# Preln linear-attention layer plus tensor-train FFN on 8 cores: stores on arrival, a shared unfold, and GpSimd's order within a slot

## The chip, the cores and the metric

The kernel runs on the 8 NeuronCores of one Trainium2 chip (trn2) as one launch. No core writes what another reads. The metric is device microseconds of the slowest core; less is better. One execution of the kernel before was profiled on all cores, and three more were timed.

## The reference, cut to what matters

Input `x` is (4, 4096, 1024) in float32. Layer norm, then an attention block with a recurrent state, a residual add, layer norm, a complex linear map whose weights come from a tensor-train product, and a second residual add:

```python
mixed = einsum('btd,cd->btc', ln(x), W_qkv)          # 3072 channels
mixed = silu(causal_conv4(mixed))                    # 4 taps per channel
q, k, v = split(mixed); q = l2norm(q) * HD**-0.5; k = l2norm(k)
z = ln(x) @ W_z.T
beta = sigmoid(ln(x) @ W_b.T)
g = -exp(A_log) * softplus(ln(x) @ W_a.T + dt_bias)
# per head and token: S = S*exp(g) + k (v*beta)^T ;  o = q S
out = rmsnorm(o) * silu(z)
x = x + out @ W_out.T
W_real = reshape(einsum('abcd,cefg->abefdg', G1_R, G2_R))   # 512 x 512, "unfold"
W_imag = reshape(einsum('abcd,cefg->abefdg', G1_I, G2_I))
x = x + [xr@W_real.T - xi@W_imag.T + br,  xr@W_imag.T + xi@W_real.T + bi]   # of ln(x)
```

## The kernel before, in words

**Who does what.** A core pair shares one of the four sequences of 4096 tokens. The even core (0, 2, 4, 6) owns the first five tiles of 512 tokens (NPRE=0, NOWN=5). The odd core first runs over the same five tiles for keys, values and state only (NPRE=5) and then owns the last three (NOWN=3). `emit(NPRE, NOWN)` builds both programs. I speak of even and odd cores.

**Slots.** The main loop runs over tiles `t` from -1 and four slots `s` in each. In a slot the core streams tile `u = t+1` (projection of a chunk of channels, the 4-tap convolution as four matmuls with diagonal blocks, SiLU), and works on chunk `n` (128 tokens) of tile `t`: decay matrix (`decay`), scores (`qk`), output (`oT`), state update (`state`). One slot later (`n1`) come `gate_out` and `outproj`, two slots later (`n2`) `ln2_norm`, `add_bias`, `ffn` and `y_store`. A slot of an even core has 7 projections and 7 convolutions (slots 0 to 2 of a tile), or 3 of both and 8 z projections (slot 3). A slot of an odd core before its own tiles has 4 and 4. The last four slots of tile `NT-1` and two more stream nothing: I call them the tail.

**Order.** Every engine takes its instructions in program order; waits are written out by hand as tokens (`need`). So the order of the calls in the slot body is the order on VectorE (`V`), GpSimd (`G`), ScalarE (`S`), TensorE (`P`) and on SyncE's DMA queue (`Y`). A `Y.need` or `G.need` holds everything that is behind it in that queue.

**Weights.** `w_uses` lists the uses of the 32 weight blocks (128x1024) in order. Five buffers `s_w` (NW=5) rotate. `w_issue(i)` loads use `i`. At the first use of a block it is a GpSimd DMA from the float32 `wcat`, which converts to bf16; it waits for the projection that last used the buffer and for the buffer's store (`q_ws`). After its first use the block lives in the bf16 scratch `wscr`, and SyncE loads it from there. `w_keep(i)` (L389) makes the store into `wscr`. In `proj(u, cc, j)` and `zproj` the order is: projection `i`, `w_keep(i)`, `w_issue(i + NW)`, then the copy of PSUM to `s_pre` (ScalarE for odd `j`, L527; VectorE for even `j`, L530). With five buffers, the load for the 7th projection of a slot is issued behind the 2nd.

**Diagonal blocks.** The same scheme with six buffers `s_d` (ND=6): at first use VectorE builds the block (L386) once the convolution that last used the buffer and the buffer's store are done. `d_keep(i)`, called behind convolution `i` (L553), stores it to `dscr`; later uses load it from there. Both stores are on SyncE's queue.

**Norms.** `ln1_norm(m)` makes the normalised rows of the tile two ahead (L431, VectorE, float32 to bf16), lets SyncE transpose them by DMA into `s_lnxT` (L140) and loads the next rows (`x_load`, 512 KB). In the slot it comes behind the fourth projection.

**Unfold.** `unfold()` builds the FFN weights `s_wbig` on VectorE: 2 parts (real, imaginary) of 4 row chunks, each 4 products (L977), 3 sums (L985) and 2 copies (L990 to L996), 72 instructions of 128x512. They are float32 but for the copies. `uf(RATE)` puts RATE of them behind each projection from slot 1 of the first tile on; RATE is 3 on even, 1 on odd cores. `xr_load` and `ffn` wait for the last one.

**GpSimd in a slot**, in order: the stores of `r_act` (row scales to `rscr`), the causal mask of the first half (`affine_select`, L756, in `decay(n,0)`), the squares of q (`s_qsq`, L791, inside `qtil`), `r_load` (two DMAs that broadcast `rscr` into `s_rb`, behind a wait for the stores), the mask of the second half, `add_bias` (L945), the state's decay (L839), small DMAs, and late in the slot the copy of the state (L875). VectorE's `gate_out` (L897) waits for `s_rb`; `outproj` waits for `gate_out` and for `s_og` (L826).

Of the kernel before, what the change touches and what calls it, by code (L numbers as in the profile page):

```python
# [8 lines left out]
ALU = mybir.AluOpType  # L9
# [139 lines left out]
def build_program():  # L149
# [93 lines left out]
    facc = x2[1][:, 512:1024]  # L243
    ftmp = x2[2][:, 0:512]
# [36 lines left out]
    def emit(NPRE, NOWN):  # L281
# [87 lines left out]
        def w_keep(i):  # L369
            u, cc = w_uses[i]  # L370
            if wscr_tok.get(cc) is None:
                Y.need(w_tok[i])
                wscr_tok[cc] = q_ws[i % NW].go(Y, wscr[cc], wr[i % NW])

        def d_issue(i):
# [8 lines left out]
            else:  # L384
# [5 lines left out]
                dscr_tok[cc] = None  # L390

        def d_keep(i):
            u, cc = d_uses[i]
            if dscr_tok.get(cc) is None:
# [113 lines left out]
        def proj(u, cc, j):  # L508
# [12 lines left out]
            w_keep(i)  # L521
# [23 lines left out]
        def conv(u, cc, j):  # L545
# [7 lines left out]
            d_keep(i)  # L553
# [13 lines left out]
        def zproj(u, cc):  # L567
            i, k, ps, t = proj_mm(u, cc)
            proj_tok[(u, cc)] = t
            w_keep(i)  # L570
# [212 lines left out]
        def qtil(n):  # L783
# [5 lines left out]
                                                 in1=eb[:, :, sl], op=ALU.mult))  # L789
            G.need(silu_tok[(t, 7)], ss_tok.get(n - 1))  # L790
# [98 lines left out]
        def r_load(n):  # L889
            G.need(q_r[0].tok, q_r[1].tok, gat_tok.get(n - 1))  # L890
# [10 lines left out]
        def xr_load(n):  # L901
            if n >= 4 * NOWN:
                return
            Y.need(yst_tok.get(n - 3), ffnw[0])
# [43 lines left out]
        def ffn(n):  # L948
            P.need(*psA_free[0])
            P.need(l2_tok[n], ffnw[0])  # L950
# [16 lines left out]
        def unfold():  # L967
            toks = [cload(Y, ft1[0], d_t1[0]), cload(Y, ft1[1], d_t1[1]),
                    cload(Y, ft2[0], d_t2[0]), cload(Y, ft2[1], d_t2[1])]
            V.need(*toks)  # L970
            t = None
            for k in range(2):
                for rc in range(4):
                    a = ft1[k][:, rc * 128:(rc + 1) * 128]
                    for c in range(4):
                        V.need(t)
                        t = V.mark(V.e.tensor_tensor(  # L977
                            out=(facc if c == 0 else ftmp).rearrange("p (b e) -> p b e", b=32),
                            in0=a[:, c * 32:(c + 1) * 32, None].broadcast_to([128, 32, 16]),
                            in1=ft2[k][:, None, c * 16:(c + 1) * 16].broadcast_to([128, 32, 16]),  # L980
                            op=ALU.mult))
                        yield
                        if c > 0:
                            V.need(t)
                            t = V.mark(V.e.tensor_tensor(out=facc, in0=facc, in1=ftmp,  # L985
# [31 lines left out]
        ffnw = [None]  # L1017
# [32 lines left out]
        for t in range(-1, NT + 1):  # L1050
            for s in range(NCH):
# [58 lines left out]
                if on2:  # L1110
                    ln2_norm(n2)
# [106 lines left out]
```

How the kernel before makes its waits and increments, by code:

```python
    def mark(self, ins):  # L110
        ins.then_inc(self.h, 1)
        self.v += 1
        return (self, self.v)
# [1 line left out]
    def need(self, *toks):  # L115
        for tok in toks:
            if tok is None:
                continue
            src, val = tok
            if val <= 0 or self.seen.get(src.name, 0) >= val:
                continue
            self.e.wait_ge(src.h, val)
            self.seen[src.name] = val
# [10 lines left out]
    def go(self, lane, out, in_):  # L134
        lane.e.dma_start(out=out, in_=in_).then_inc(self.h, 16)
        self.v += 16
        return (self, self.v)
# [1 line left out]
    def gotr(self, lane, out, in_):  # L139
        lane.e.dma_start_transpose(out=out, in_=in_).then_inc(self.h, 16)
        self.v += 16
        return (self, self.v)
# [122 lines left out]
    def begin(eng, name, out, in_):  # L265
        eng.dma_start(out=out, in_=in_).then_inc(sem(name), 16)
        begun.add(name)
```

## Time and profile before

| what | value |
|---|---|
| runs of the kernel before | 893.12, 892.51, 887.84 us; median 892.51 |
| the profiled execution's own time | 892.11 us |
| its span, slowest core (core 2, even) | 890.2 us |
| spans, even cores 0, 2, 4, 6 | 888.1, 890.2, 886.6, 879.7 us |
| spans, odd cores 1, 3, 5, 7 | 882.8, 886.2, 887.3, 881.4 us |
| core 2, busy | PE 77%, VectorE 55%, ScalarE 33%, GpSimd 30% |
| core 2, DMA | 129 MB, mean 145 GB/s |

The span runs from a core's first to its last instruction; the execution's own time is 1.9 us above the span of the slowest core. Times in the rows are microseconds from the start of the core's span. PE is TensorE, DVE VectorE, ACT ScalarE, POOL GpSimd, SPq SyncE's DMA queue. "PEclk" is TensorE's granted clock as a share of full speed, "DMA share" the mean busy share of 16 DMA engines. In a row of the timeline the bracket holds the idle time of the engine before the instruction and what ended it. DMA-issuing rows show the issue, not the transfer.

### The profile page before, as it was taken

What the parts mean: (1) busy time and instruction counts of PE and PEld (TensorE: products, weight loads), DVE (VectorE), ACT (ScalarE), POOL (GpSimd) and SP (SyncE); (2) the same over time, 40 slices, a digit from 0 to 9 for tenths busy, and PEclk for the clock granted to TensorE, in tenths of its full rate; (3) what the DMA queues carried; (4) which work ended last, traced back from release to release, by engine and by line L of the source; (5) the groups of instructions that cost most, each with busy time, mean ns of one, the idle gap of its engine ahead of it and who ended that gap; (6) DMA issues with size and microseconds to landing.
All of it is one profiled execution on the core that took longest, in us unless ns stands there. A gap on an engine that the chain in (4) does not pass through costs nothing.

```text
span 890.2 us, 14242 instructions; the slowest of 8 cores (879.7 to 890.2 us)
## 1 busy us (share of the span) xinstructions
PE 686.3 (77%) x4687; PEld 316.4 (36%) x4767; DVE 487.2 (55%) x678; ACT 296.8 (33%) x522; POOL 266.9 (30%) x317
## 2 busy tenths in 40 slices
PE   0768674689887979979897997897999897665543
PEld 0323231234343424434343443443444443332211
DVE  4537784245656365666546657633465453656532
ACT  1143340246434325433434444413543343111100
POOL 2122111033324150450514315325044152334410
PEclk9998896799998989999899999989999999766668
DMA  9598986876366663744746456365374464122222
GB/s 195 118 238 168 182 198 184 200 205 188 78 181 171 156 175 100 203 129 152 193 132 193 122 176 168 105 169 136 116 190 105 106 163 109 41 77 67 84 59 63
DMA packets 102223, 129.00 MB, mean 145 GB/s; under 512 B 48382, under 2 KB 65284, under 8 KB 102016
## 3 DMA queue, kind: packets, MB, share of 16 engines
q1 hardware_dynamic: 88272, 99.38, 39.2%
q0 software_dynamic: 13872, 28.63, 16.7%
q8 instruction: 42, 0.69, 0.3%
q14 instruction: 37, 0.30, 0.1%
HBM read 107.40 MB, written 22.76 MB: 146 GB/s over the span
## 4 chain that ended last, share of the span: by engine, by line
PE 53%; DMA 20%; DVE 11%; issue 7%; ACT 4%; SPq 2%; POOL 2%; DVEq 0%; ACTq 0%; POOLq 0%
PE pR L503 20%; PE pR L550 9%; PE pB L912 9%; PE pA L953 7%; DMA dscr<-s_d 6%; DMA s_w<-wscr 5%; DMA wscr<-s_w 3%; DMA s_rb<-rscr 3%; DVE s_ln L935 2%; SPq L140 1%; DMA s_i128b<-i 1%; PE pB L807 1%; DMA rscr<-s_r 1%; PE pB L813 1%; DVE s_ktil L728 1%
## 5 line engine op out<-in xcount | busy, mean ns | idle before, releaser
L503 PE MATMUL pR<-s_lnxT,s_w 128*128 128x512 bf16 x1240 | 314.7, 405 | 73.2 <-DMA s_w<-wscr 27.3
L503 PEld LDWEIGHTS pR<-s_lnxT,s_w 128*128 128x128 bf16 x1280 | 126.9, 102 | 239.7 <-issue 115.7
L550 PE MATMUL pR<-s_pre,s_d 128*128 128x512 bf16 x460 | 117.1, 386 | 15.7 <-DVE s_pre L530 9.3
L135 POOL DMA_DIRECT2D rscr<-s_r x40 | 22.2, 558 | 267.4 <-ACT s_r L884 92.1
L912 PE MATMUL pB<-s_wout,s_gated 128*128 128x512 bf16 x308 | 80.7, 416 | 23.5 <-DVE s_og L826 11.6
L556 ACT ACTIVATE s_post<-pR 128x512 bf16<-128x512 f32 x120 | 68.9, 593 | 64.1 <-PE pR L550 63.6
L530 DVE CAST s_pre<-pR 128x512 bf16<-128x512 f32 x70 | 48.0, 688 | 70.1 <-PE pR L503 70.1
L918 DVE TENSOR_TENSOR s_x<-pB,s_x 128x1024 f32<-128x1024 f32 x20 | 24.5, 1225 | 101.2 <-PE pB L912 101.2
L953 PE MATMUL pA<-s_wbig,s_ln2T 128*128 128x512 bf16 x312 | 73.2, 384 | 6.6 <-DMA s_ln2T<-s_ln 6.1
L550 PEld LDWEIGHTS pR<-s_pre,s_d 128*128 128x128 bf16 x480 | 41.6, 98 | 64.5 <-issue 19.7
L527 ACT CAST s_pre<-pR 128x512 bf16<-128x512 f32 x50 | 29.3, 585 | 96.2 <-PE pR L503 96.1
L573 ACT ACTIVATE s_zT<-pR 128x512 bf16<-128x512 f32 x40 | 23.7, 597 | 110.2 <-PE pR L503 100.3
L912 PEld LDWEIGHTS pB<-s_wout,s_gated 128*128 128x128 bf16 x320 | 33.2, 106 | 66.9 <-issue 36.8
L875 POOL CAST s_Sb<-s_S 128x512 bf16<-128x512 f32 x20 | 12.2, 608 | 146.3 <-DVE s_ssb L870 146.3
L556 ACT ACT_TABLE_LOAD x20 | 25.7, 1283 | 77.6 <-PE pR L550 77.6
L756 POOL TENSOR_SCALAR_AFFINE_SELECT s_dsb<-s_dsb 128x1024 bf16<-128x1024 bf16 x40 | 44.4, 1110 | 23.6 <-ACT s_dsb L752 23.1
L414 ACT ACT_TABLE_LOAD x21 | 26.9, 1283 | 71.1 <-DVE s_pre L480 58.5
L135 POOL DMA_DIRECT2D s_w<-wcat x31 | 17.2, 557 | 101.0 <-DMA wscr<-s_w 38.8
L953 PEld LDWEIGHTS pA<-s_wbig,s_ln2T 128*128 128x128 bf16 x320 | 31.3, 99 | 44.6 <-issue 8.3
L958 DVE TENSOR_TENSOR s_x<-pA,s_x 128x1024 f32<-128x1024 f32 x20 | 24.5, 1225 | 41.1 <-PE pA L953 41.1
L945 POOL TENSOR_TENSOR s_x<-s_x,s_biasb 128x1024 f32<-128x1024 f32 x20 | 42.6, 2129 | 14.2 <-DVE s_ln L935 14.2
L897 DVE TENSOR_TENSOR s_gated<-s_og,s_rb 128x1024 bf16<-128x1024 bf16 x20 | 25.0, 1250 | 29.5 <-DMA s_rb<-rscr 29.5
(118 smaller groups left out, 891.7 us busy)
## 6 DMA issues: line engine op xcount, KB each, us to landing
s_w<-wscr SPq DMA_DIRECT2D x128, 256.0 KB, 4.6
s_d<-dscr SPq DMA_DIRECT2D x96, 128.0 KB, 3.4
s_x<-x SPq DMA_DIRECT2D x22, 512.0 KB, 5.7
s_rb<-rscr POOLq DMA_DIRECT2D x40, 256.0 KB, 4.7
y<-s_x SPq DMA_DIRECT2D x20, 512.0 KB, 2.9
s_xa<-x SPq DMA_DIRECT2D x18, 512.0 KB, 6.4
s_w<-wcat POOLq DMA_DIRECT2D x32, 256.0 KB, 6.2
wscr<-s_w SPq DMA_DIRECT2D x32, 256.0 KB, 5.6
```

The costliest lines, as they stand in the source:

```text
L135: lane.e.dma_start(out=out, in_=in_).then_inc(self.h, 16)
L414: t = S.mark(S.e.activation(out=bn[:, 14:15], in_=bn[:, 13:14], func=AF.Ln, bias=EPS5))
L503: ins = P.e.matmul(ps, w[:, dc * 128:(dc + 1) * 128], lnxT[u % 2][:, dc, :], start=(dc == 0), stop=(dc == 7))
L527: te = S.mark(S.e.copy(out=pre[:, j, 3:515], in_=ps))
L530: te = V.mark(V.e.tensor_copy(out=pre[:, j, 3:515], in_=ps))
L550: ins = P.e.matmul(ps, dr[i % ND][:, tap * 128:(tap + 1) * 128], pre[:, j, tap:tap + 512], start=(tap == 0), stop=(tap == 3))
L556: silu_tok[(u, cc)] = ring_free[k] = S.mark(S.e.activation(out=post[u % 2][:, cc, :], in_=ps, func=AF.Silu))
L756: exp_tok[(n, h2)] = G.mark(G.e.affine_select(out=d3, in_=d3, pattern=[[0, 8], [1, 128]], compare_op=ALU.is_ge, fill=zero_reg, base=0, cha ...
L897: gat_tok[n] = V.mark(V.e.tensor_tensor(out=gated.rearrange("p (a b) -> p a b", a=8), in0=og.rearrange("p (a b) -> p a b", a=8), in1=rb, o ...
L912: ins = P.e.matmul(pB[:, hf * 512:(hf + 1) * 512], gated[:, cc * 128:(cc + 1) * 128], wout[:, cc, hf * 512:(hf + 1) * 512], start=(cc == 0 ...
L945: xb_tok[n] = G.mark(G.e.tensor_tensor(out=x2[n % 3], in0=x2[n % 3], in1=biasb, op=ALU.add))
L953: ins = P.e.matmul(pA[:, hf * 512:(hf + 1) * 512], ln2T[n % 2][:, dg, :], wbig[:, dg, hf * 512:(hf + 1) * 512], start=(dg == 0), stop=(dg ...
```

## The change

Five edits.

1. `d_keep` is gone: the block is stored to `dscr` right behind its building, in `d_issue`.
2. `w_keep` is called two uses ahead (`i + 2`) in `proj` and `zproj`, and for uses 0 and 1 before the first norms.
3. `unfold(L, k)` is now one generator for each part: part 0 on VectorE, part 1 on GpSimd, with buffers of their own (part 1 borrows half of an `s_x2` buffer and half of `s_rb`). `uf` steps both. RATE for even cores is 2. The loads of its inputs are issued at the end of slot 0. `r_load`, `xr_load` and `ffn` wait for both parts.
4. `ln1_norm` moves from behind the fourth projection to directly behind `ln2_norm`, between the first and the second projection.
5. GpSimd's squares of q leave `qtil` and become `q_squares`, called behind `qk(n, 1)`; `add_bias` is moved there too, behind them.

```diff
-    facc = x2[1][:, 512:1024]
-    ftmp = x2[2][:, 0:512]
+    facc = [x2[1][:, 512:1024], x2[2][:, 512:1024]]
+    ftmp = [x2[2][:, 0:512], rb.rearrange("p a b -> p (a b)")[:, 0:512]]
...
         def w_keep(i):
+            if i not in w_tok:
+                return
             u, cc = w_uses[i]
-            if wscr_tok.get(cc) is None:
+            if wscr_tok[cc] is None:
                 Y.need(w_tok[i])
                 wscr_tok[cc] = q_ws[i % NW].go(Y, wscr[cc], wr[i % NW])
...
                     in1=cw[:, cc, :, None].broadcast_to([128, 4, 128]), op=ALU.mult))
-                dscr_tok[cc] = None
-
-        def d_keep(i):
-            u, cc = d_uses[i]
-            if dscr_tok.get(cc) is None:
                 Y.need(d_tok[i])
                 dscr_tok[cc] = q_ds[i % ND].go(Y, dscr[cc], dr[i % ND])
...
-            w_keep(i)
+            w_keep(i + 2)
             w_issue(i + NW)
...
-            d_keep(i)
             d_issue(i + ND)
...
+        def q_squares(n):
+            t, c = NPRE + n // 4, n % 4
+            sl = slice(c * 128, (c + 1) * 128)
             G.need(silu_tok[(t, 7)], ss_tok.get(n - 1))
             qsq_tok[n] = G.mark(G.e.tensor_tensor(out=qsq, in0=post[t % 2][:, 0:8, sl],
                                                   in1=post[t % 2][:, 0:8, sl], op=ALU.mult))
...
-            G.need(q_r[0].tok, q_r[1].tok, gat_tok.get(n - 1))
+            G.need(q_r[0].tok, q_r[1].tok, gat_tok.get(n - 1), ffnw[1])
...
-            Y.need(yst_tok.get(n - 3), ffnw[0])
+            Y.need(yst_tok.get(n - 3), *ffnw)
...
+        def unfold(L, k):
+            L.need(*t_ft)
+            t, acc, tmp = None, facc[k], ftmp[k]
+            for rc in range(4):
+                a = ft1[k][:, rc * 128:(rc + 1) * 128]
+                for c in range(4):
+                    L.need(t)
+                    t = L.mark(L.e.tensor_tensor(
+                        out=(acc if c == 0 else tmp).rearrange("p (b e) -> p b e", b=32),
+                        in0=a[:, c * 32:(c + 1) * 32, None].broadcast_to([128, 32, 16]),
+                        in1=ft2[k][:, None, c * 16:(c + 1) * 16].broadcast_to([128, 32, 16]),
+                        op=ALU.mult))
+                    yield
+                    if c > 0:
+                        L.need(t)
+                        t = L.mark(L.e.tensor_tensor(out=acc, in0=acc, in1=tmp, op=ALU.add))
                         yield
...
+                yield
+            ffnw[k] = t
+
+        unfolding = []
 
         def uf(k):
             for _ in range(k):
-                if unfolding[0] is not None and next(unfolding[0], "over") == "over":
-                    unfolding[0] = None
+                for g_ in list(unfolding):
+                    if next(g_, "over") == "over":
+                        unfolding.remove(g_)
...
+        w_keep(0)
+        w_keep(1)
...
-        RATE = 3 if NPRE == 0 else 1
+        RATE = 2 if NPRE == 0 else 1
...
                 if on2:
                     ln2_norm(n2)
+                ln1_norm(m)
                 fe(1)
                 if own:
                     decay(n, 0)
                     qtil(n)
                 fe(2)
-                ln1_norm(m)
                 if on1:
                     r_load(n1)
                 if own:
                     decay(n, 1)
-                if on2:
-                    add_bias(n2)
...
                 if own:
                     qk(n, 1)
+                if own:
+                    q_squares(n)
+                if on2:
+                    add_bias(n2)
                 if on1:
                     gate_out(n1)
...
                 if t == -1 and s == 0:
-                    unfolding[0] = unfold()
+                    t_ft += [cload(Y, ft1[0], d_t1[0]), cload(Y, ft1[1], d_t1[1]),
+                             cload(Y, ft2[0], d_t2[0]), cload(Y, ft2[1], d_t2[1])]
+                    unfolding += [unfold(V, 0), unfold(G, 1)]
```

## Rows read from the trace of the kernel before

**Rows 1.** Busy time by stretch: core 2, then core 3
```profile
core 2: us, PE busy (x) PEld busy (x) DVE busy (x) ACT busy (x) POOL busy (x), PEclk, DMA share, GB/s
28.00:167.00 139.00, 92.70 (x383) 36.46 (x393) 79.98 (x149) 40.87 (x70) 24.31 (x44) 0.88 0.84 182
200.00:700.00 500.00, 442.70 (x3150) 206.39 (x3207) 287.77 (x373) 201.33 (x354) 166.51 (x186) 0.96 0.56 153
...
35.00:123.00 88.00, 52.15 (x250) 20.94 (x243) 33.74 (x71) 31.98 (x55) 9.61 (x17) 0.83 0.79 155
430.00:470.00 40.00, 18.05 (x71) 6.61 (x72) 2.14 (x5) 4.41 (x8) 7.05 (x11) 0.68 0.78 171
```
**Rows 2.** Waits of core 2, whole span: us in total, times, longest
```profile
POOL s_w L135 <- DMA wscr<-s_w: 38.8, 6, 17.7
DVE s_d L386 <- DMA dscr<-s_d: 20.7, 6, 7.4
```
**Rows 3.** Timeline of core 2, first tile
```profile
53.99 3.97 DVE L386 TENSOR_TENSOR s_d<-s_i128f,s_cw 128x512 bf16<-128x512 f32 x6 [7.45 <-DMA dscr<-s_d]
62.72 0.69 DVE L386 TENSOR_TENSOR s_d<-s_i128f,s_cw 128x512 bf16<-128x512 f32 x1 [4.76 <-DMA dscr<-s_d]
64.86 0.68 DVE L530 CAST s_pre<-pR 128x512 bf16<-128x512 f32 x1
152.88 3.20 PE L503 MATMUL pR<-s_lnxT,s_w 128*128 128x512 bf16 x8 [11.58 <-DMA s_w<-wcat]
```
**Rows 4.** Costs by shape, core 2: unfold on VectorE, nearest form on GpSimd
```profile
L977 DVE TENSOR_TENSOR s_x<-s_x 128x512 f32<-128x512 f32 x32 | 22.1, 690 | 2.6
L839 POOL TENSOR_TENSOR s_S<-s_S,s_gam 128x512 f32<-128x512 f32 x20 | 20.8, 1042 | 0.1
```
**Rows 5.** Timeline: VectorE beside GpSimd, core 3, then core 2
```profile
418.24 1.05 POOL L839 TENSOR_TENSOR s_S<-s_S,s_gam 128x512 f32<-128x512 f32 x1
418.27 1.59 DVE L386 TENSOR_TENSOR s_d<-s_i128f,s_cw 128x512 bf16<-128x512 f32 x1
...
357.99 3.61 DVE L431 TENSOR_SCALAR s_lnx<-s_xa,s_bnA 128x1024 bf16<-128x1024 f32 x1
359.14 1.90 POOL L791 TENSOR_TENSOR s_qsq<-s_post 128x1024 bf16<-128x1024 bf16 x1
```
**Rows 6.** Timeline of core 2, SyncE's queue in a steady slot
```profile
356.91 1.25 SPq L140 DMA_TRANSPOSE s_ln2T<-s_ln  x1
358.25 1.48 SPq L135 DMA_DIRECT2D s_w<-wscr  x3
361.67 1.23 SPq L140 DMA_TRANSPOSE s_lnxT<-s_lnx  x1
362.96 0.58 SPq L135 DMA_DIRECT2D s_xa<-x  x1
```
**Rows 7.** DMA issues of core 2 at 358.3 and at 399.0: size, us to landing
```profile
s_w<-wscr SPq DMA_DIRECT2D x1, 256.0 KB, 3.8
...
s_w<-wscr SPq DMA_DIRECT2D x1, 256.0 KB, 5.7
```
**Rows 8.** Waits of core 2, 200 to 700 us
```profile
PE pR L503 <- DMA s_w<-wscr: 23.0, 7, 3.8
PE pB L807 <- DVE s_dsb L777: 9.2, 6, 2.2
```
**Rows 9.** Timeline of core 2, one slot of the tail
```profile
773.24 1.18 POOL L135 DMA_DIRECT2D rscr<-s_r  x2 [9.37 <-ACT s_r L884]
776.90 2.32 POOL L791 TENSOR_TENSOR s_qsq<-s_post 128x1024 bf16<-128x1024 bf16 x1
779.17 1.12 POOL L135 DMA_DIRECT2D s_rb<-rscr  x2
785.35 1.23 DVE L897 TENSOR_TENSOR s_gated<-s_og,s_rb 128x1024 bf16<-128x1024 bf16 x1 [2.60 <-DMA s_rb<-rscr]
```
**Rows 10.** Chain that ended last, core 2, the same slot: start us, us
```profile
773.88 2.93 DMA rscr<-s_r
```

More of the change, by code:

```diff
@@ L569, in zproj @@
             proj_tok[(u, cc)] = t
-            w_keep(i)
+            w_keep(i + 2)
             w_issue(i + NW)
@@ L949, in ffn @@
             P.need(*psA_free[0])
-            P.need(l2_tok[n], ffnw[0])
+            P.need(l2_tok[n], *ffnw)
             for dg in range(8):
@@ L964, in y_store @@
             yst_tok[n] = q_y[n % 3].go(Y, y[n * 128:(n + 1) * 128, :], x2[n % 3])
[L967 to L981, printed above, removed]
-                        yield
-                        if c > 0:
-                            V.need(t)
-                            t = V.mark(V.e.tensor_tensor(out=facc, in0=facc, in1=ftmp,
-                                                         op=ALU.add))
-                            yield
-                    V.need(t)
-                    if k == 0:
-                        V.e.tensor_copy(out=wbig[:, rc, 0:512], in_=facc)
-                        yield
-                        t = V.mark(V.e.tensor_copy(out=wbig[:, 4 + rc, 512:1024], in_=facc))
-                    else:
-                        V.e.tensor_copy(out=wbig[:, rc, 512:1024], in_=facc)
-                        yield
-                        t = V.mark(V.e.tensor_scalar(out=wbig[:, 4 + rc, 0:512], in0=facc,
-                                                     scalar1=-1.0, scalar2=None, op0=ALU.mult))
-                    yield
-            ffnw[0] = t
@@ L1001, in emit @@
-        unfolding = [None]
+        t_ft = []
+        def unfold(L, k):
[14 more added lines that the diff above has]
+                        t = L.mark(L.e.tensor_tensor(out=acc, in0=acc, in1=tmp, op=ALU.add))
+                        yield
+                L.need(t)
+                if k == 0:
+                    L.e.tensor_copy(out=wbig[:, rc, 0:512], in_=acc)
+                    yield
+                    t = L.mark(L.e.tensor_copy(out=wbig[:, 4 + rc, 512:1024], in_=acc))
+                else:
+                    L.e.tensor_copy(out=wbig[:, rc, 512:1024], in_=acc)
+                    yield
+                    t = L.mark(L.e.tensor_scalar(out=wbig[:, 4 + rc, 0:512], in0=acc,
+                                                 scalar1=-1.0, scalar2=None, op0=ALU.mult))
+                yield
+            ffnw[k] = t
@@ L1015, in emit @@
         t_bonesq = cload(G, bonesq.rearrange("p a b -> p (a b)"), d_bonesq)
+        w_keep(0)
+        w_keep(1)
         late = {}
-        ffnw = [None]
+        ffnw = [None, None]
         ln1_stats(0)
```

## The prediction

> **What bounds the kernel now.** I read the spans of the cores first. All eight lie within 879.7 to 890.2 us, odd and even alike, so a gain counts only if both programs have it. The slowest is an even core (core 2), whose terms I work out; the odd ones come after.
>
> The second view is busy time by stretch [rows 1]. From 200 to 700 us TensorE is busy 442.7 of 500 us at clock 0.96: that part is bound by TensorE, with some 57 us of gaps. In the first tile (28 to 167) it is busy 92.7 of 139 us, at clock 0.88. The DMA share there is 0.84, so 139 x 0.84 = 117 us of transfer time is in it: if the same bytes move at the same price, this stretch can't shrink by more than 22 us.
>
> The waits say what fills the gaps [rows 2]: VectorE waits 20.7 us to build diagonal blocks until their stores land, GpSimd 38.8 us for stores of weights before it issues the next load. The timeline shows how [rows 3]. The block at 53.99 waits 7.45 us, that at 62.72 another 4.76 us, and behind it in VectorE's queue stands the first PSUM copy of the next slot (64.86), which TensorE needs. The stores were late because `d_keep` stands behind the convolution, and on SyncE's queue behind the slot's stores of weights. Late in the tile one projection waits 11.58 us for a load that waited for such a store.
>
> In the tail nothing streams, and a slot is a chain of latencies: rows to `rscr`, back into `s_rb`, `gate_out`, `outproj`, residual, norm. There GpSimd's order counts [rows 9, 10]: the two stores are issued from 773.24 to 774.42, a transfer of them takes 2.93 us, so both have landed by about 777.4, but the load stands behind the squares of q and goes out at 779.17; `gate_out` then waits 2.60 us for it.
>
> **Edits 1 and 2, stores on arrival.** They remove no bytes and add no instruction. Stores of blocks go out right behind the building, 15 us before they are needed, so VectorE's waits go. Slot 0 has no unfold work, so its gain is plain: the first copy of slot 1 at 64.86 comes down to about 55, when the seventh block needs no wait. That is 10 us. For the later slots I take 4 us of the remaining 8.5 us of such waits (20.7 - 7.45 - 4.76), since the unfold lies beside them, and 4 us of the 11.58 us wait near the end: the load goes out earlier, but it meets a busy DMA. What is late next is the transfers themselves, hence the ceiling of 22. From below: the two early `w_keep` stand before the loads of rows on SyncE and hold them until the second weight block has landed. A transfer of that size takes 4 to 6 us [rows 7], so at worst 3 us lost at the start. I take +18 for the two, bounds -3 and +22.
>
> **Edit 3, the shared unfold.** VectorE loses 36 of 72 instructions: 28 x 0.69 = 19.3 us and 8 copies of under 0.69 each, about 23 us. GpSimd gets 28 x 1.04 = 29.1 us and 8 copies of at most 1.04, 29 to 37 us; I take 34, copies being the simpler work [rows 4]; it has this time, being busy 24.3 of 139 us. But the two engines hinder each other [rows 5]. The building of a block takes 0.69 us alone, and 1.59 us where it starts beside GpSimd's 1.05 us product: it ends 0.57 us behind GpSimd's end. And `ln1_norm`, 0.8 us alone, takes 3.61 us, until 0.56 us behind the end of GpSimd's squares. So VectorE stood through GpSimd's instruction, and in the second case through two in a row. If each of the 36 new ones did that, VectorE would lose 34 us where it saves 23, a loss of 11 us; if none, it gains 23 but shows it only as far as VectorE holds TensorE up. Half of 34 is 17, so I expect the saving spent, and take -2. Bounds: -13 (11, and 2 for loads that stand behind GpSimd's pair of instructions) and +4, what the DMA ceiling leaves.
>
> The Trainium skill says this as a rule (SBUF — State Buffer, section "SBUF: two separate sides"): the port pair that VectorE and GpSimd share is an exclusive lock for the whole instruction, taken against VectorE when it runs a two-port mode or has two SBUF inputs. The rows agree, and by the rule nearly every unfold instruction of one engine excludes that of the other. Its sum is the first rival below.
>
> First tile: 18 - 2 = **16 us less**, of a ceiling of 22.
>
> **Edit 4, the earlier norm.** It stands now before the second projection, so on SyncE the transpose (1.23 us) and the load of rows (0.58 us) come ahead of the load that is issued behind that projection. That load serves the seventh projection of the slot. Today it goes out at 358.25 and lands in 3.8 us; a load behind a transpose and a 512 KB load of rows took 5.7 us [rows 6, 7]. So it lands 1.2 + 0.6 + 1.9 = 3.7 us later. This is felt already: TensorE waits 23.0 us, 7 times, for such loads [rows 8]. Tile by tile, core 2 norms during three tiles of its own, with three slots of 7 projections each: 9 slots. In about half of them `ln2_norm` (1.9 to 2.1 us beside the squares, else 0.8) now ends 1.2 us earlier, since the squares are gone from there. The mean loss per slot lies between 0 (the slack of the slots that don't wait today) and 3.7; I take 1.5, as the later waits absorb some: 9 x 1.5 = 13.5 us more, bounds 0 and 33.
>
> **Edit 5, GpSimd's order.** In the steady stretch the masks come 2 us earlier and VectorE's norm no longer stands beside the squares. Waits that this may shorten: 9.2 us for the masked scores [rows 8] and as much again for PSUM copies and the like. I take 6.5 us less, bounds +0 and -18. On the other side the squares (1.9) and the bias (2.1, back to back) now lie where `halo_out`, `qk` and `gate_out` run on VectorE; this is harmless only as long as VectorE reads PSUM then. I price that at 0 in the forecast and give it a rival.
>
> In the tail the load of `s_rb` can go out at 777.4 instead of 779.17: 1.8 us in this slot. Two more slots show the same with 2.1 to 2.2 us, the first only 0.5 us. The squares are then needed by `state` some 4 us later, which they meet. Sum **6 us less**, bounds 2 (if `gate_out` meets the bias) and 8.
>
> **The sum.** Core 2: 892.1 (the profiled execution, 1.9 above its span) - 16 + 13.5 - 6.5 - 6 = **877.1 us**. The median of the runs shown is 892.51, so the same to 0.4 us.
>
> Odd cores: first tile 88 us with a DMA share of 0.79 [rows 1], ceiling 18, I take 12. At 430 to 470 they load their remaining weights with TensorE busy 18 of 40 us and DMA 0.78, ceiling 9, I take 5. Own slots with a norm and 7 projections: 6, so 9 us more; tail 6 less. Core 3 comes to 886.2 + 1.9 - 12 - 5 + 9 - 6 = 874, so the even cores set the time.
>
> **The rivals.**
> *The shared unfold eats the first tile's gain.* One VectorE instruction waits for each of GpSimd's: edit 3 costs 34 - 23 = 11, and the later slots' and the load's gain (8) doesn't show because VectorE is the bound: 10 - 11 = -1. For it: VectorE is busy 80 of 139 us there, and every copy of TensorE's results to `s_pre` with even `j` waits in its queue. Against it: GpSimd lags on loads, so the pairs don't always meet. Time: 892.1 + 1 + 13.5 - 6.5 - 6 = **894**.
>
> *DMA fills up and VectorE is freed.* First tile at its ceiling (-22), the early norm hidden by slack (+3), VectorE's relief -8, tail -7: **858**. For it: GpSimd waits 38.8 us for stores in the first tile. Against it: the wait of 23 us for the second load shows that slack is thin.
>
> *VectorE stands behind squares and bias (slower).* Place: the middle of each streaming slot of an own tile, 16 on core 2. The two run 4.0 us back to back; `halo_out` or `gate_out` that starts beside the first is held until the end of both, and the scores behind it, for which `oT` on TensorE waits. Price 0 to 4 us per slot. My forecast has 15 us to lose, so from 0.9 us per slot the change is no gain, and from 1.5 us it is slower by 1%. At 1.8 us it gives 877 + 29 = **906**. For it: 3.61 us in [rows 5] is just such a wait. Against it: most of VectorE's work there reads PSUM, and I found no copy from PSUM that grew beside GpSimd.
>
> **How the numbers follow.** Forecast (868 to 890) 0.50, the DMA ceiling 0.20, the eaten gain 0.18, the held VectorE 0.12. A measurement of this kernel tells about 1% from no change, that is 883.6 and 901.4 us. Of the forecast 0.37 lies below 883.6 and 0.13 within 1%; the second rival is all below (0.20) and the first within (0.18); the third is 0.10 above and 0.02 within. That gives 0.57 faster, 0.33 the same, 0.10 slower. The range 860 to 900 takes in all but half of the second rival and most of the third.
>
> **What would show it.** Right: no VectorE wait for `dscr` stores, and GpSimd's wait for `wscr` stores under 10 us; the first copy of slot 1 near 55 us; the second tile starting 12 to 20 us earlier; tail slots of 23 to 24 us instead of 25 to 27; the wait of TensorE for `s_w` from `wscr` grown from 23 to 30 us or more. Wrong: unfold products on VectorE with a mean over 1.2 us and the second tile starting where it did (first rival); DMA share over 0.95 in the first tile (second); `halo_out` or `gate_out` with a mean over 2.5 us and TensorE's gaps from 200 us on grown by more than 15 us (third).

## The result and the profile after: 2.2% slower

The changed kernel takes **911.25 us** (median; the profiled execution 908.54) against 891.07 us for the kernel before beside it: ratio 1.022, 95% interval 1.018 to 1.026. Forecast were 877.1 us, range 860 to 900, with 0.10 for slower. The forecast failed. One of the four executions was disturbed and is left out of the ratio.

The spans of the cores come first (span, mean granted clock). Cores 4 to 7 repeat the pattern, with core 6 the slowest at 906.6 us:

```profile
core 0: 905.3 us, clock 0.897
core 1: 870.8 us, clock 0.917
core 2: 899.4 us, clock 0.910
core 3: 860.4 us, clock 0.914
```

The kernels have parted. Even cores are 9 to 27 us slower than in the kernel before, odd cores 12 to 34 us faster. The even ones set the time.

To see where, I split the span of each even core at the start of the gate computation of each tile (VectorE's first operation on `s_gt`, L600 before, L596 after) and take the mean of the four even cores. What lies ahead of the first such operation, 33.6 us before and 33.9 after, has no column:

| us, mean of cores 0, 2, 4, 6 | first tile | tiles 2 to 4 | last tile and tail | span |
|---|---|---|---|---|
| before | 140.3 | 433.0 | 279.2 | 886.2 |
| after | 131.2 | 459.8 | 279.1 | 904.0 |
| difference | -9.1 | +26.8 | -0.1 | +17.8 |
| forecast | -16 | +7 | -6 | |

(Two profiles of one identical kernel, in the last experiments, differ by 1.4, 6.2 and 1.2 us in these columns, so a difference of 5 us in one column is not told from none.)

**First tile.** Busy time by stretch, core 2 then core 3, columns as in [rows 1]:

```profile
28.00:167.00 139.00, 94.38 (x424) 37.74 (x421) 85.77 (x115) 43.97 (x76) 70.14 (x80) 0.89 0.87 191
200.00:700.00 500.00, 436.31 (x3081) 198.75 (x3080) 241.00 (x363) 191.63 (x337) 160.54 (x179) 0.95 0.55 147
...
35.00:123.00 88.00, 65.26 (x371) 27.72 (x370) 51.14 (x80) 42.02 (x71) 36.62 (x40) 0.86 0.91 193
```

GpSimd went from 24 to 70 us busy in core 2's first stretch. Yet VectorE, which gave 36 instructions away, rose from 80 to 86. From 200 to 700 us TensorE lost 6 us of busy time, and VectorE fell from 288 to 241 us (on core 4 the two norms alone fell from 52.4 to 19.4). So edit 5's relief of VectorE is there, but VectorE does not bound this part, and little of it reached TensorE. Waits of core 2 over its whole span, then the timeline of its slot 1 [rows 2, 3]:

```profile
POOL s_w L135 <- DMA wscr<-s_w: 9.1, 4, 3.4
DVE s_d L388 <- DMA dscr<-s_d: 7.4, 1, 7.4
```
```profile
54.93 0.69 DVE L388 TENSOR_TENSOR s_d<-s_i128f,s_cw 128x512 bf16<-128x512 f32 x1 [0.52 <-PE pR L547]
63.01 0.69 DVE L388 TENSOR_TENSOR s_d<-s_i128f,s_cw 128x512 bf16<-128x512 f32 x1 [7.39 <-DMA dscr<-s_d]
...
65.16 0.68 DVE L527 CAST s_pre<-pR 128x512 bf16<-128x512 f32 x1
```

The waits shrank (38.8 to 9.1 and 20.7 to 7.4), but the first copy of slot 1, forecast near 55, starts at 65.16 where it started at 64.86. SyncE's queue says why:

```profile
39.76 17.70 SPq L135 DMA_DIRECT2D wscr<-s_w  x6
57.55 6.55 SPq L135 DMA_DIRECT2D dscr<-s_d  x7
```

In the kernel before, the blocks' stores were issued from 43.76 on. Now `w_keep(i + 2)` waits for a load of weights that has not landed, and the stores of blocks stand behind it in that queue until 57.55. On core 2 the second tile starts only 3.8 us earlier (its gate computation at 166.8 instead of 170.6), where 12 to 20 were forecast. The instructions of the unfold and the builds in core 2, each form by itself [rows 4]:

```profile
L388 DVE TENSOR_TENSOR s_d<-s_i128f,s_cw 128x512 bf16<-128x512 f32 x24 | 21.8, 950 | 9.4 <-DMA dscr<-s_d 7.4 <-PE pR L547 1.9
L977 DVE TENSOR_TENSOR s_x<-s_x 128x512 f32<-128x512 f32 x16 | 18.3, 1145 | 6.7 <-DMA s_x<-t2i 5.8
L985 POOL TENSOR_TENSOR s_x<-s_x,s_rb 128x512 f32<-128x512 f32 x12 | 17.2, 1430 | 1.0
L977 POOL TENSOR_TENSOR s_rb<-s_x 128x512 f32<-128x512 f32 x12 | 14.4, 1204 | 1.0
```

VectorE's products take 1145 ns where they took 690, its block builds 950 where all 24 took 687 before. GpSimd's products take 1204 and its sums 1430, where its nearest row, a product, was 1042. On the other even cores VectorE's products take 907 to 1117 ns.

**Steady tiles.** Waits of TensorE in core 2, 200 to 700 us [rows 8], then a slot of core 4 in the timeline, then the DMA issues of that core between 392 and 400 us (KB each, median us to landing), then its busy time in two stretches:

```profile
PE pR L500 <- DMA s_w<-wscr: 37.5, 9, 7.7
PE pB L807 <- DVE s_dsb L773: 8.8, 5, 2.8
```
```profile
392.57 0.81 DVE L428 TENSOR_SCALAR s_lnx<-s_xa,s_bnA 128x1024 bf16<-128x1024 f32 x1
392.73 1.23 SPq L140 DMA_TRANSPOSE s_ln2T<-s_ln  x1
...
394.05 2.33 SPq L140 DMA_TRANSPOSE s_lnxT<-s_lnx  x1
394.73 1.89 PE L500 MATMUL pR<-s_lnxT,s_w 128*128 128x512 bf16 x8 [0.33 <-DVE s_pre L527]
...
396.44 0.58 SPq L135 DMA_DIRECT2D s_xa<-x  x1
397.11 10.65 SPq L135 DMA_DIRECT2D s_w<-wscr  x6
403.79 3.56 PE L500 MATMUL pR<-s_lnxT,s_w 128*128 128x512 bf16 x8 [7.18 <-DMA s_w<-wscr]
```
```profile
s_w<-wscr SPq DMA_DIRECT2D x5, 256.0 KB, 7.0
...
s_xa<-x SPq DMA_DIRECT2D x1, 512.0 KB, 6.2
```
```profile
395.00:404.00 9.00, 1.82 (x9) 0.66 (x8) 0.65 (x2) 0.59 (x1) 7.62 (x9) 0.80 1.12 207
404.00:408.00 4.00, 4.00 (x18) 1.32 (x17) 0.54 (x1) 0.00 (x0) 0.00 (x0) 0.60 0.45 166
```

The norm is done at 393.4, and in 0.81 us, its time alone. But two transposes and a load of 512 KB now stand ahead of the weights: the first of these goes out at 397.11, 4.38 us behind the first transpose, where it went out 1.34 us behind it [rows 6]. The loads of this stretch land in 7.0 us (median) instead of 3.8 and 5.7 [rows 7], with a DMA share of 1.12 from 395 to 404 us, and TensorE waits 7.18 us. Behind the gap the granted clock is 0.60 in the mean of 4 us, between TensorE's two levels of 1.2 and 2.4 GHz, and the eight matmuls behind it take 3.56 us, where eight of the same form took 1.89 ahead of it.

**Tail.** One slot of core 2 [rows 9]:

```profile
789.43 1.22 POOL L135 DMA_DIRECT2D s_rb<-rscr  x2
...
793.47 1.90 POOL L791 TENSOR_TENSOR s_qsq<-s_post 128x1024 bf16<-128x1024 bf16 x1
...
794.71 3.84 DVE L897 TENSOR_TENSOR s_gated<-s_og,s_rb 128x1024 bf16<-128x1024 bf16 x1 [1.58 <-DMA s_rb<-rscr]
...
795.32 2.13 POOL L945 TENSOR_TENSOR s_x<-s_x,s_biasb 128x1024 f32<-128x1024 f32 x1
```

`gate_out` waits 1.58 us instead of 2.60, and then takes 3.84 us instead of 1.23, until 1.1 us behind the end of GpSimd's second instruction. Not every slot does so: later in the same tail, at 845.80, the gating takes 1.24 us again.

### The profile page after: what moved, and what is told of

Same layout as the page of the kernel before. It is cut to its first block, busy times and chain, and to the rows that moved or that the text cites. A ratio compares the mean times of both kernels' runs of the same rounds, so it can differ in the third digit from the quotient of the medians.

```text
span 906.6 us, 14273 instructions; the slowest of 8 cores (853.4 to 906.6 us)
## 1 busy us (share of the span) xinstructions
PE 687.0 (76%) x4687; PEld 316.0 (35%) x4767; DVE 455.0 (50%) x642; ACT 296.1 (33%) x522; POOL 313.5 (35%) x353
## 4 chain that ended last, share of the span: by engine, by line
PE 40%; DMA 22%; DVE 16%; issue 10%; ACT 5%; SPq 3%; POOL 2%; DVEq 0%; ACTq 0%; POOLq 0%
PE pR L500 11%; PE pB L912 9%; PE pR L547 9%; DMA s_w<-wscr 9%; PE pA L953 6%; DMA s_rb<-rscr 5%; DMA rscr<-s_r 2%; SPq L140 2%; DMA wscr<-s_w 2%; ACT L411 2%; DVE s_gated L897 2%; DVE s_d L388 1%; DMA s_w<-wcat 1%; DMA s_i128b<-i 1%; DVE s_lnx L428 1%
## 5 line engine op out<-in xcount | busy, mean ns | idle before, releaser
L547 PE MATMUL pR<-s_pre,s_d 128*128 128x512 bf16 x460 | 119.4, 392 | 15.1 <-DVE s_pre L527 11.0
L897 DVE TENSOR_TENSOR s_gated<-s_og,s_rb 128x1024 bf16<-128x1024 bf16 x20 | 30.0, 1498 | 40.6 <-DMA s_rb<-rscr 40.6
L791 POOL TENSOR_TENSOR s_qsq<-s_post 128x1024 bf16<-128x1024 bf16 x20 | 38.0, 1901 | 0.3
```

The costliest lines, as they stand in the source:

```text
L547: ins = P.e.matmul(ps, dr[i % ND][:, tap * 128:(tap + 1) * 128], pre[:, j, tap:tap + 512], start=(tap == 0), stop=(tap == 3))
L791: qsq_tok[n] = G.mark(G.e.tensor_tensor(out=qsq, in0=post[t % 2][:, 0:8, sl], in1=post[t % 2][:, 0:8, sl], op=ALU.mult))
L897: gat_tok[n] = V.mark(V.e.tensor_tensor(out=gated.rearrange("p (a b) -> p a b", a=8), in0=og.rearrange("p (a b) -> p a b", a=8), in1=rb, o ...
```

## The experiments

All ratios are to the kernel before, run on the same chip in turn, with 95% intervals; 1% is 9 us. Waits are those of TensorE in core 4 from 200 to 700 us; stretches are means of the even cores, as in the table above. "Changed" is the kernel after.

### Which edit costs

**e1_norm_back**: changed, edit 4 undone.
```diff
                     ln2_norm(n2)
-                ln1_norm(m)
                 fe(1)
...
                 fe(2)
+                ln1_norm(m)
```


> The changed kernel with the norm of the tile two ahead put back behind the fourth projection; stores on arrival, the shared unfold and GpSimd's new order stay. Theory A (the early norm puts a transpose and a 512 KB load ahead of the weight load that the seventh projection needs): core 0's waits of TensorE for s_w from wscr fall from 46.5 us to 25 or less, the tiles two to four of the even cores lose the 9 to 15 us each that they gained in length, and the time is 870 to 885 us. Rival B (the squares and the bias in the middle of the slot hold VectorE): the waits for s_w fall, but the tiles stay long, 895 to 905 us. Rival C (the shared unfold is what costs): within 5 us of the changed kernel, 906 to 916 us.

Measured 886.34 us, ratio 0.994 (0.990 to 0.997), just above the 885 of theory A. Without edit 4 the change would have been a small gain; edit 4 costs 1.022 - 0.994 = 2.9%, 25 us. Its streamed tiles take 433.2 us against 459.8, as in the kernel before.

**e2_norm_alone**: before, with edit 4 alone.
```diff
                     ln2_norm(n2)
+                ln1_norm(m)
                 fe(1)
...
                 fe(2)
-                ln1_norm(m)
```


> The kernel before with the early norm alone. Theory A: slower than the kernel before by 20 to 35 us on the even cores (910 to 925 us), by 5 to 15 us on the odd ones, whose own tiles are fewer; no change in the first tile. Rival B: within 8 us of the kernel before, since the squares and the bias are where they were.

Measured 932.91 us, ratio 1.048 (1.042 to 1.054), above the 925 of theory A. Its first tile, where no change was expected, takes 146.4 us instead of 140.3, and TensorE waits 33.2 us for PSUM copies on core 4, more than for weights (13.5). So theory A is not the whole of it; e12 below takes it apart.

**e3_stores_alone**: before, with edits 1 and 2. Its diff is the part of the change on `w_keep` and `d_keep`.

> The kernel before with the stores on arrival alone (both kinds). Theory A gives these the whole gain of the first tile: even cores 12 to 18 us shorter, odd cores 20 to 28 us, time 870 to 882 us. Rival D (the shared unfold is needed for the gain, since VectorE bounds the first tile with all 72 unfold instructions): even cores at most 8 us shorter, 882 to 890 us.

Measured 872.76 us, ratio 0.978 (0.972 to 0.985). Run again later as **e17_stores_again**:

> Stores on arrival alone once more, beside the two halves of edit 5: 0.9784 of the time before, between 0.973 and 0.984, and the fastest of these kernels unless one half of edit 5 is a gain.

870.31 us, ratio 0.975 (0.971 to 0.979). The first tile takes 121.5 and 122.9 us instead of 140.3, the other stretches stay. Busy time of core 2 in its first tile, and two waits of its whole span:

```profile
28.00:155.00 127.00, 96.45 (x431) 38.61 (x431) 80.74 (x150) 40.97 (x71) 24.22 (x44) 0.85 0.98 205
```
```profile
POOL s_w L135 <- DMA wscr<-s_w: 64.0, 11, 9.2
...
DVE s_d L388 <- DMA dscr<-s_d: 7.4, 2, 6.9
```

The DMA share is 0.98: the stretch is at its ceiling. GpSimd waits for stores longer than before (64.0 against 38.8 us), which fits transfers as the new bound. Most of the gain sits in one place, the last slot of the tile. Its first three projections, its last two, and the gates behind them, in the kernel before and then in e3, core 2:

```profile
117.28 5.34 PE L503 MATMUL pR<-s_lnxT,s_w 128*128 128x512 bf16 x23
...
161.07 5.94 PE L503 MATMUL pR<-s_lnxT,s_w 128*128 128x512 bf16 x16 [4.99 <-DMA s_w<-wcat]
166.94 0.63 PE L587 MATMUL pG<-s_lnxT,s_wab 128*32 128x128 bf16 x32
```
```profile
117.22 5.34 PE L500 MATMUL pR<-s_lnxT,s_w 128*128 128x512 bf16 x23
...
147.97 6.48 PE L500 MATMUL pR<-s_lnxT,s_w 128*128 128x512 bf16 x16 [3.77 <-DMA s_w<-wcat]
154.38 0.63 PE L583 MATMUL pG<-s_lnxT,s_wab 128*32 128x128 bf16 x32
```

Both reach this slot at 117.2 us. Behind it e3 is 12.6 us ahead (on the other even cores 3 to 4 us are gained ahead of the slot and 15 to 18 in it; the next tile's first load from `wscr` then takes 5 to 9 us of waiting back), and TensorE's waits for loads from `wcat` are 12.3 us instead of 22.6 (core 2, 28 to 170 us).

**e5_order_alone**: before, with edit 5.
```diff
-                if on2:
-                    add_bias(n2)
                 if streaming and s == 2:
                     gates_d(u)
...
                     qk(n, 1)
+                if own:
+                    q_squares(n)
+                if on2:
+                    add_bias(n2)
```


> The kernel before with the squares of q and the bias moved behind the scores, alone. Theory A: faster by 5 to 15 us, of it 4 to 7 in the tail (r_load no longer stands behind the squares) and the rest from a VectorE whose norm no longer stands beside the squares: 876 to 886 us. Rival B: slower, 893 to 905 us, with gate_out or halo_out means over 2 us.

Measured 896.10 us, ratio 1.004 (1.001 to 1.008): the rival's range, not theory A's.

**e9_stores_order**: edits 1, 2 and 5 together; **e13_stores_unfold**: edits 1, 2 and 3; **e4_unfold_back**: changed, with both parts of the unfold on VectorE, RATE 3:
```diff
-                    unfolding += [unfold(V, 0), unfold(G, 1)]
+                    unfolding += [unfold_both()]
```


> The kernel before with edits 1, 2 and 5 (stores on arrival, GpSimd's long work in the second part of a slot), without the shared unfold and without edit 4. If the edits add up as measured alone (0.9784 and 1.0044 of the time before): 875 to 877 us. If edit 5 costs more once the first tile is shorter: up to 886, which would leave nothing for edit 3. If edit 5 gives something then, 868 or less, and all the difference to the run with edit 4 undone (886.3) is edit 3's.

> Stores on arrival plus the shared unfold (edits 1, 2 and 3), with neither edit 4 nor edit 5. By difference of two runs (0.9936 with edits 1, 2, 3 and 5, 0.9875 with 1, 2 and 5) edit 3 costs 0.6%: 0.984 to 0.987, some 878 us. If edit 3 costs only where GpSimd's squares stand in the second part of a slot: 0.978. If it gives something without edit 5: below 0.975.

> The changed kernel with the unfolding of the first tile back on VectorE alone (both parts one after the other, a copy of the same code); edits 1, 2, 4 and 5 stay. Theory A (the unfold on GpSimd slows VectorE's block builds, 964 ns where they took 687, and is worth +5 to +9 us of the even cores, the difference left between the run with edit 4 undone, 886.3, and stores alone, 872.8, less edit 5's own 0 to 4): 903 to 906 us, and the builds in the first tile near 700 ns. Theory B (GpSimd's half is a gain, as the prediction's range allowed to 13 us, and the missing microseconds come from edit 5 alone): 915 us or more. If edit 3 is nothing, 911.

Measured: e9 882.69 us, 0.988 (0.982 to 0.993). e13 881.95 us, 0.986 (0.979 to 0.993). e4 906.73 us, 1.015 (1.009 to 1.020). In e4 the block builds are back at 687 ns, and the time is within 1 us of theory A's range. With stores alone at 0.977 (mean of its two runs):

- edit 3 costs 0.986 - 0.977 = 0.9% on top of the stores, 0.994 - 0.988 = 0.6% beside edit 5 (e1 against e9), and 1.022 - 1.015 = 0.8% in the changed kernel (against e4). Each difference alone is near its interval; all three agree on 5 to 8 us. In the column of the first tile they are 11 (133.6 against 122.2 us), 6 (128.2 against 122.2) and 4 us (131.2 against 127.1).
- edit 5 costs 0.4% alone and 1.1% on top of the stores, there in tiles 2 to 4 (442.0 against 433.7 us) and in the last column (280.1 against 276.3).

### How edit 4 costs

**e6_norm_behind_second**: changed, the norm and its two transfers one projection later. **e7_norm_early_send_late**: changed, VectorE's norm where edit 4 put it, SyncE's transpose and `x_load` at the old place. **e14_transpose_early_x_late**: changed, only `x_load` at the old place.
```diff
 e6              fe(1)
+                ln1_norm(m)
...
 e7              fe(2)
+                ln1_send()      # Y.need, transpose, x_load(m + 2)
...
 e14             fe(2)
+                x_late()        # x_load(m + 2)
```


> The changed kernel with the ln1 norm and its two transfers moved from ahead of the second projection to directly behind it, so that SP issues that projection's weight load ahead of the DMA transpose. Theory A (edit 4 costs through SP's order: the transpose and the x load stand ahead of the load that the seventh projection waits for, 37.8 us of such waits on core 4 between 200 and 700 us): the wait for weights falls back to some 17 us there and the time to 886 to 892 us, that of edit 4 undone. Theory B (it costs because VectorE's norm stands too early, beside GpSimd's work and ahead of the PSUM copies): the time stays within 5 us of 911, and the wait for weights turns into one for the copy.

> The changed kernel with VectorE's norm left where edit 4 put it, but with SP's transpose and x load issued only at their old place. Theory A (SP's order): 884 to 892 us, with the wait for weights near 17 us between 200 and 700 us on core 4. Theory B (VectorE's placement): above 905 us.

> The changed kernel with the DMA transpose where edit 4 put it, and only SP's x load (512 KB) back at its old place. Both back gave 0.9938 of the time before, against 1.0222 for the change. If the transpose is the cost (two in a row ahead of the weight loads, which then stand behind their small packets): 1.012 or more. If the x load is: 0.994 to 1.002. If each carries its share: 1.002 to 1.012.

| | us | ratio | waits for weights | tiles 2 to 4 |
|---|---|---|---|---|
| changed | 911.25 | 1.022 | 37.8 | 459.8 |
| e14, transpose early, x load late | 892.95 | 1.002 (0.999 to 1.004) | 28.9 | 445.1 |
| e7, both late, norm early | 887.74 | 0.994 (0.991 to 0.997) | 19.9 | 438.1 |
| e6, all behind the second projection | 884.03 | 0.992 (0.988 to 0.995) | 18.5 | 434.2 |
| e1, edit 4 undone | 886.34 | 0.994 | 16.3 | 433.2 |

In the changed kernel SyncE's order is the whole loss. Where VectorE does the norm is worth nothing here (e7 against e1). Of the 2.8% between e7 and the changed kernel, the x load carries 2.0% (with the transpose early) and the transpose 0.8% (with the x load late). One projection later, behind one weight load, neither costs anything (e6). The rows of waits, of the changed kernel, e14 and e7:

```profile
PE pR L500 <- DMA s_w<-wscr: 37.8, 9, 7.2
```
```profile
PE pR L505 <- DMA s_w<-wscr: 28.9, 8, 6.1
```
```profile
PE pR L508 <- DMA s_w<-wscr: 19.9, 6, 5.5
```

In e14, in the slot that answers to the one shown, the first load goes out at 387.51 with no 512 KB ahead; the weights issued in that stretch land in 5.3 us, not 7.0. Over tiles 2 to 4 of core 4 the median landing moves less, 4.2 us before and 4.8 in the changed kernel: the long landings are those of the stretch behind the norm.

**e12_norm_alone_send_late**: the kernel before with VectorE's norm early and SyncE's two transfers late, to see whether e2's 4.8% has the same cause. **e10_stores_norm_second**: stores alone with e6's place of the norm.

> The kernel before with edit 4's norm on VectorE, but with SP's transpose and x load at their old place. Edit 4 alone with its transfers cost 4.8%, and there the projections waited for VectorE's PSUM copy (33.2 us on core 4 between 200 and 700 us) more than for weights (13.5). Theory A (the transfers' place in SP's queue is the whole cost, and the late copies are its consequence): 888 to 898 us, within 1% of the time before. Theory B (in this kernel, where GpSimd's squares and bias sum stand in the first part of the slot, VectorE's norm is itself what delays the copies): 920 us or more.

> Stores on arrival (the kernel before with edits 1 and 2, 0.9784 of the time before) with the ln1 norm and its transfers directly behind the second projection, not the fourth. Theory A (what counts is only whether the transpose stands ahead of the second projection's weight load): 0.973 to 0.983 of the time before. If an earlier place is worth something once it is behind that load, as 884.0 against 886.3 us in the changed kernel hints: 0.970 to 0.976. If earlier is worse in steps: 0.985 or more.

Measured: e12 902.44 us, 1.011 (1.003 to 1.019), between its two theories. e10 895.11 us, 1.005 (1.003 to 1.008), 2.8% above stores alone: theory A is out, and of the three ranges only "earlier is worse" (0.985 or more) holds it. SyncE's order is 1.048 - 1.011 = 3.7 of e2's 4.8%, with 17.4 us of waits for weights over tiles 2 to 4 against 6.3. The rest, and e10's loss, is another mechanism. Waits and VectorE's groups of e10:

```profile
PE pR L500 <- DVE s_pre L527: 33.2, 9, 6.1
```
```profile
L784 DVE TENSOR_TENSOR s_eb<-s_post,s_eb 128x1024 bf16<-128x1024 bf16 x13 | 19.9, 1533 | 0.0
L428 DVE TENSOR_SCALAR s_lnx<-s_xa,s_bnA 128x1024 bf16<-128x1024 f32 x10 | 19.0, 1903 | 0.0
```

The norm takes 1.9 us, `qtil` behind it 1.53 us instead of 0.68, and TensorE waits 33.2 us for PSUM copies that stand behind the two in VectorE's queue (7.8 us in the kernel before, 4.3 in e6). In these two kernels GpSimd's squares still stand in the first part of the slot. Late, behind the copies, the norm takes 3.1 us in stores alone (core 4) and no wait for copies grows; early, it holds them. The streamed tiles show the same price in both: 453.3 against 436.8 and 430.6 for stores alone, 450.7 against 433.0. So edit 5 is what makes an early norm harmless on VectorE: with it the norm takes 0.81 us in e6, `qtil` 0.69, and the tiles 434.2 us. (e6 has edit 3 too, which works in the first tile only.) That e12 as a whole lost less than e10 comes from its first tile (129.7 against 140.3 us), which I have not explained.

**e11_stores_send_last**: stores alone, with the transpose and x load behind all projections of the slot's first part.
```diff
                 fe(8)
+                ln1_send()
```


> Stores on arrival with SP's transpose and x load moved behind the last front projection of the slot, behind all its weight loads; VectorE's norm stays. Theory A (each transpose ahead of a weight load costs): the waits for weights on core 4 between 200 and 700 us fall from 18.0 us to under 8, and the time to 855 to 866 us (0.96 to 0.97). Rival (the remaining waits come from the second layer norm's transpose or the loads' own length, and the late transpose is waited for by the next tile): no gain, 872 us, or a loss.

Measured 878.52 us, 0.987 (0.980 to 0.994). A miss, and 1.0% slower than stores alone: the waits for weights are 20.6 us, not under 8. The transfers of the norm are not what those remaining waits come from; what is stays open.

### Which half of edit 5 costs

**e15_stores_squares_moved** moves only the squares, **e16_stores_bias_moved** only `add_bias`, each on top of stores alone.

> Stores on arrival with only the squares of q moved behind the second qk (half of edit 5). Both halves cost some 0.9% on top of stores. Theory A (VectorE's halo copy and output gating now stand beside the squares, 1.9 us alone): 0.983 to 0.988 of the time before, and the halo copy's mean above 1000 ns on core 4 between 200 and 700 us, where it is 680. Theory B (the bias sum is what disturbs): 0.976 to 0.980.

> Stores on arrival with only the bias sum moved behind the second qk (the other half of edit 5). Theory A (the squares are the cost): 0.974 to 0.980, and the ln1 norm, which takes 3089 ns on core 4 beside the bias sum, falls below 2000 ns. Theory B: 0.983 or more.

e15: 877.46 us, 0.978 (0.975 to 0.982). e16: 877.30 us, 0.982 (0.979 to 0.984). Beside them e17 gave 0.975. Neither half is a gain; the bias costs some 0.6%, the squares 0.3%, within their interval. The halo copy of 21 elements per partition from 200 to 700 us, core 4, this form alone, in the kernel before, in e9, in e15 and in e16:

```profile
L486 DVE COPY s_halo<-s_pre 128x21 bf16<-128x21 bf16 x11 | 3.5, 317 | 1.1
```
```profile
L483 DVE COPY s_halo<-s_pre 128x21 bf16<-128x21 bf16 x11 | 18.1, 1646 | 1.1
```
```profile
L483 DVE COPY s_halo<-s_pre 128x21 bf16<-128x21 bf16 x11 | 17.7, 1613 | 1.1
```
```profile
L483 DVE COPY s_halo<-s_pre 128x21 bf16<-128x21 bf16 x11 | 7.7, 704 | 1.1
```

The copy takes 1646 ns where it took 317, and TensorE's wait for masked scores rises from 8.2 to 18.0 us in e9 (16.1 in e15, 12.4 in e16). Theory A of e15 had the copy right and the time wrong: with a mean of 1613 ns e15 loses little, and e16, where it is 704, loses no less. So the slower copy is seen, but it is not shown to be the price of edit 5.

TensorE's waits over tiles 2 to 4, mean of the even cores, in stores alone (mean of e3 and e17, which differ by up to 0.9 us in one kind and 2.4 in all) and in e9, say more:

| us | masked scores | `s_og` | PSUM copies | all waits | tiles 2 to 4 |
|---|---|---|---|---|---|
| stores alone | 9.0 | 0.5 | 6.4 | 49.9 | 433.7 |
| e9 | 13.2 | 7.6 | 2.2 | 56.6 | 442.0 |

The relief came, 4 us at the PSUM copies. It is outweighed by 4 us at the masked scores and 7 us at `s_og`, which VectorE makes behind `gate_out`. `gate_out` itself takes no longer in these tiles (1216 ns on core 4 in e9, 1255 in e3), but it waits longer for the load of `s_rb`: 27.3 us instead of 8.5, and that load lands in 6.7 us (median, core 4, 200 to 600 us) instead of 4.3. In e5 it is 6.2 against 5.0 in the kernel before, in e15 and e16, with one half each, 4.5. Why it lands later no run here tells.

The Trainium skill (SBUF — State Buffer, section "SBUF: two separate sides") calls the pair of ports between VectorE and GpSimd an exclusive lock for the whole instruction. The halo copy (1646 against 317 ns), the gating at 794.71 (3.84 against 1.23 us) and the unfold (1145 against 690 ns) agree with it. What the rows add is that the loser may stand through two GpSimd instructions in a row, as the 3.84 us did.

## Why the prediction was wrong, point by point

**Edits 1 and 2: right in size, wrong in place.** Forecast -18, measured -2.3% = -20 us, all in the first tile. The step that put 10 of these at the first copy of slot 1 failed: "stores go out right behind the building" overlooked `w_keep(i + 2)` ahead of them in SyncE's queue. Most of the gain came in the tile's last slot instead, 12.6 us on core 2 where the forecast had 4, up to a DMA share of 0.98. That the total came out right is luck. The second rival said the first tile would reach its ceiling (-22), and without the other edits it came near it.

**Edit 3: the term was mis-sized.** Forecast +2, measured +5 to +8, between forecast and first rival (+11). "Half of 34" was too little: the VectorE instructions given away came back as slower ones. The mean of the 16 products rose by 455 ns, that of 24 builds by 263 (core 2).

**Edit 4: the loss per slot was mis-sized, forecast +13.5, measured +25.** The mechanism was the right one: weight loads that stand behind the norm's transfers. The term of 1.5 us per slot failed. On core 2 from 200 to 700 us TensorE's waits for weights rose from 23.0 to 37.5 us, 14.5 against 13.5 forecast, but this agreement is luck. Over tiles 2 to 4 and all even cores they are 20.2 us before, 42.0 in the changed kernel and 18.2 with edit 4 undone (e1). So edit 4 brought 23.8 us in nine slots, 2.6 per slot. The slot shown above tells why: its load goes out 4.38 instead of 1.34 us behind the first transpose and lands in 7.0 instead of 3.8 us, 6.2 us later where the forecast had 3.7. All waits of TensorE in these tiles are 48.0 us in e1 and 69.7 in the changed kernel, so 22 of the 27 us between the two are waits.

The sum also left out what follows a wait. After 7.18 us of idling the granted clock was 0.60 and eight matmuls took 3.56 us. Over tiles 2 to 4 of core 4 (174.0 to 606.2 us before, 163.8 to 623.4 after) TensorE's granted clock is 0.97 before and 0.94 after:

```profile
174.00:606.20 432.20, 377.80 (x2749) 176.93 (x2800) 255.12 (x331) 174.78 (x308) 139.92 (x157) 0.97 0.59 160
```
```profile
163.80:623.40 459.60, 394.00 (x2823) 180.27 (x2824) 219.27 (x330) 174.57 (x308) 141.00 (x157) 0.94 0.58 151
```

That is 137.4 and 139.6 ns per matmul, so by estimate 2823 x 2.2 ns = 6 us of the 27 come with the lower clock. The same estimate from the means of the even cores, 138.7 ns in e1 and 140.2 in the changed kernel, gives 4 us. It is the smaller part. The effect was in the trace of before, behind most waits for weights (on core 2 at 247.56 eight matmuls took 3.44 us behind a wait of 3.11), and I priced each at its idle time alone. I also took the transpose as the main obstacle; the x load is, at 2.0 of 2.8%.

**Edit 5: the step that failed most, the sign was wrong.** Forecast -6.5 in the steady part and -6 in the tail, with the squares and the bias in the middle of the slot priced at 0; measured +0.4% alone and +1.1% on top of the stores. The relief of VectorE came, but less: 4 us at the PSUM copies. The waits for masked scores, which were to shrink, grew by 4 us, and those for `s_og` by 7 (e9 against stores alone). The price of 0 rested on "harmless only as long as VectorE reads PSUM then", and the halo copy and the gating read no PSUM. How much of the loss is theirs stays open: of the two halves, the copy grew more in the one that cost less (e15), and the later landing of `s_rb` stands beside it. The third rival named this place at 29 us; edit 5 cost 4 to 10 net. In the tail the earlier load saved 1.0 us of waiting in the slot shown and the slower gating took 2.6 us back.

**The sum.** By the runs: -20 (stores), +7 (unfold), +8 (order), +25 (norm) = +20, with edits 3 and 5 as the mean of both orders in which they were added. That this is what was measured follows from the way it is added up, step by step from the kernel before to the changed one. The forecast's -15 is 35 us off: -2 on the stores, +5 on edit 3, +20 on edit 5 and +12 on edit 4. So edit 5 held the largest error, though edit 4 holds the largest loss and the second largest error.

**Odd cores.** Forecast 874, measured 853 to 871 (mean 860): stores on arrival are worth more there (847 with stores alone), and edit 4 costs 13 us where 9 were forecast.

The best kernel of all is before with edits 1 and 2 alone, 870 to 873 us, 2.2 to 2.5% under the kernel before. Nothing that was put on top of it made it faster; moving the squares alone (0.978) is not told from it.

## What to carry to other kernels

Before moving an instruction earlier, list what it sends to each queue and what stands behind: with edit 5 in place the norm itself was free at its new place, its 512 KB load ahead of a weight load was not (2.0%). Without edit 5 the norm was not free either (e10). Price a gap in TensorE's work at more than its length, and read the price from the matmuls that follow an existing gap of the same kind. Offloading to GpSimd, and moving its long instructions, here moved the collision with VectorE instead of removing it; look for what on VectorE reads and writes SBUF at the new place, down to copies of 21 elements. And read a mean by shape: with two shapes in one row the halo copy stood at 678 ns in the kernel before, where the common shape took 317. Last, a match between a forecast term and one core's window is no proof of the term: take all cores and the run with the edit undone.

## What the runs showed of the hardware that I had not expected

- A gap of 7.18 us is followed by eight matmuls in 3.56 us instead of 1.89, with a granted clock of 0.60 between 404 and 408 us.
- With two transposes and a 512 KB load issued just ahead, 256 KB weight loads landed in 7.0 us instead of 3.8, and in 5.3 us without the 512 KB load (e14). The mean DMA share over three tiles was 0.58, but 1.12 from 395 to 404 us: the transfers bunch in a short stretch that the mean hides.
- A 128x21 copy on VectorE, 280 ns where it meets nothing, had a mean of 1215 ns beside GpSimd's squares and bias sum (core 4, whole span of e3 and e1, this form alone).
- The two engines slow each other: GpSimd's float32 product of 128x512 took 1204 ns beside VectorE's unfold, and the nearest product of the same size 1042 ns elsewhere (core 2), while VectorE's went from 690 to 1145 ns.
